# One transposition and four transfers for each unit's maxima, and the last unit's staging two slots later

## The reference, cut to what matters

```python
# x: (2, 512, 128); context: (2, 32, 128); 16 heads of 64
ln = layernorm(layernorm(x));  xn = layernorm(context)
q  = rmsnorm(ln @ Wq) * scale                 # per head
k, v = concat([xn @ Wkv, ln @ Wkv])           # 32 context keys + 512 own keys
attn = softmax(q @ k.T)                       # (2, 16, 512, 544)
x  = x + tanh(g_xattn) * ((attn @ v) @ Wout + bout)
# then 8 experts, top 2 of them, each silu(y @ W_gate) * (y @ W_up) @ W_down
x  = x + tanh(g_ffn) * experts(layernorm(x))
```

## Time and profile before

| | |
|---|---|
| time of three runs, median | 338.35 us (338.27 to 339.49) |
| time of the profiled execution | 338.54 us |
| its span | 336.7 us |
| PE busy | 295.9 us, 88% |
| DVE busy | 276.1 us, 82% |
| POOL busy | 267.5 us, 79% |
| ACT busy | 203.4 us, 60% |
| mean granted clock of PE | 0.976 |

### The profile page before, as it was taken

The page is one execution under the profiler, slowest core; times in us unless marked ns, Lnnn a source line. Parts: engine busy times, 40 slices in busy tenths (PEclk is TensorE's granted clock), DMA queues, the critical chain, the costliest instruction groups (busy, mean ns, idle before and its releaser), DMA issues.

```text
span 336.7 us, 8703 instructions
## 1 busy us (share of the span) xinstructions
PE 295.9 (88%) x3313; PEld 182.0 (54%) x3313; DVE 276.1 (82%) x524; ACT 203.4 (60%) x353; POOL 267.5 (79%) x202
## 2 busy tenths in 40 slices
PE   0466578899999999999999999899988899999993
PEld 0243243455556555565555656677865675655552
DVE  3898888899899898998998986964727976898995
ACT  2463756768756765766766656466673557665551
POOL 8699897897998999999989987545973449677662
PEclk9996969999999999999999999999999999999998
DMA  6405326343514516306308159360100000001001
GB/s 169 136 22 132 67 39 128 43 115 86 122 34 88 126 30 138 84 18 154 75 15 188 51 146 189 102 182 2 45 6 3 0 3 0 2 3 32 2 0 33
DMA packets 33865, 23.63 MB, mean 70 GB/s; under 512 B 10976, under 2 KB 33312, under 8 KB 33824
## 3 DMA queue, kind: packets, MB, share of 16 engines
q1 hardware_dynamic: 32880, 23.03, 29.3%
q10 hardware_dynamic: 944, 0.04, 0.2%
HBM read 5.88 MB, written 0.52 MB: 19 GB/s over the span
## 4 chain that ended last, share of the span: by engine, by line
POOL 34%; PE 24%; issue 20%; DVE 16%; ACT 4%; DMA 1%; POOLq 1%; DVEq 0%; ACTq 0%
POOL p_lo L602 14%; POOL rms_r L501 7%; POOL p_lo L637 7%; PE pj L1348 4%; DVE nm_main L1000 3%; PE big L1537 3%; PE big L1538 2%; PE o_ps L1377 2%; PE tv L1331 2%; PE o_ps L1371 1%; POOL x_sb L647 1%; PE o_ps L1372 1%; DVE wqkv_hl L1238 1%; POOL ln_r L490 1%; DVE qk L981 1%
## 5 line engine op out<-in xcount | busy, mean ns | idle before, releaser
L602 POOL TENSOR_TENSOR p_lo<-p 128x1024 f16<-128x1024 f32 x64 | 121.8, 1915 | 12.8 <-ACT p L798 12.8
L798 ACT ACTIVATE p<-big 128x1024 f32<-128x1024 f32 x64 | 65.6, 1025 | 42.6 <-PE big L1538 42.5
L1000 DVE TENSOR_REDUCE nm_main<-big 128x2 f32<-128x1024 f32 x64 | 78.1, 1220 | 14.1 <-PE big L1396 13.8
L501 POOL TENSOR_TENSOR rms_r<-meansq,power 128x8 f32<-128x8 f32 x32 | 52.3, 1638 | 11.4 <-DVE meansq L974 11.3
L637 POOL TENSOR_TENSOR p_lo<-p,p_lo 128x512 f16<-128x512 f32 x32 | 37.1, 1159 | 30.1 <-ACT p_lo L879 29.2
L1537 PE MATMUL big<-w 128*128 128x512 f16 x128 | 48.8, 381 | 1.9 <-ACT p L798 1.6
L1538 PE MATMUL big<-w 68*128 68x512 f16 x128 | 48.7, 380 | 0.0
L1371 PE MATMUL o_ps<-v,p 128*128 128x65 f16 x512 | 40.3, 193 | 0.0
L1372 PE MATMUL o_ps<-v,p 128*128 128x64 f16 x512 | 40.2, 194 | 0.0
L1371 PEld LDWEIGHTS o_ps<-v,p 128*128 128x128 bf16 x512 | 35.6, 99 | 6.7 <-issue 3.4
L1372 PEld LDWEIGHTS o_ps<-v,p 128*128 128x128 bf16 x512 | 34.1, 97 | 3.1
(11 more groups left out here) (226 smaller groups left out, 713.3 us busy)
## 6 DMA issues: line engine op xcount, KB each, us to landing
w<-hl SPq DMA_DIRECT2D x32, 256.0 KB, 4.1
w<-hl SPq DMA_DIRECT2D x32, 128.0 KB, 3.7
pc_st<-pc_hi SPq DMA_DIRECT2D x64, 32.0 KB, 1.9
pc_st<-pc_lo SPq DMA_DIRECT2D x32, 32.0 KB, 1.8
hl<-n_kernel_gating_EDF_dram SPq DMA_DIRECT2D x1, 1024.0 KB, 6.4
hl<-L_ffn_kernel_up_EDF_dram SPq DMA_DIRECT2D x1, 1024.0 KB, 5.7
o_sb<-in_L_xattn_Wkv_dram SPq DMA_DIRECT2D x2, 384.0 KB, 7.2
x_sb<-in_x_dram SPq DMA_DIRECT2D x2, 256.0 KB, 4.1
```

The lines of the kernel that those rows point to most:

```text
L501: nc.gpsimd.tensor_tensor(rms_r[:, tau % QT, :], meansq[:, tau % QT, :], power[:, 0:8], ALU.pow).then_inc(rr_ok, 1)
L602: nc.gpsimd.tensor_tensor(p_lo[m % NP][:, :], p[m % NP][:, :], p_hi[m % NP], ALU.subtract).then_inc(plo_ok, 1)
L798: nc.scalar.activation(p[n % NP][:, :], st_ps, ACT.Exp).then_inc(exp_ok, 1)
L1000: nc.vector.tensor_reduce(nm_main[:, u % 2, 2 * c:2 * c + 2, q], s2_ps.rearrange("p (k n) -> p k n", k=2), AX_X, ALU.max, negate=True).the ...
```

## The change

`nm16` is turned by one transposition of 128 x 16 in place of four of 128 x 4. The result has 16 rows (4 blocks x 4 heads) of 128, and `nmT` is a tensor of 16 rows; ACT copies 16 x 128 in place of 4 x 512. As the four blocks now lie on different partitions, SP spreads them with four transfers in place of one, and all waits on `sh_ok` count four times as much. Besides, the staging of unit 7 moves from slot 48 to slot 50. In SP's list it comes then behind the stack of unit 6 (slot 49) and still ahead of the transfer of `wd` (slot 51).

```diff
-        nmT = sb("nmT", [HG, QT, P], F16)
+        nmT = sb("nmT", [QT * HG, P], F16)
-        W_AT = {(FIRST, -1)[u] if u < 2 else 8 * u - 8: u for u in range(UNITS)}
+        W_AT = {(FIRST, -1)[u] if u < 2 else 8 * u - (8 if u < UNITS - 1 else 6): u for u in range(UNITS)}
...
-                    sp.dma_start(W2[u % 2][DH:M_ROWS, 2:4, :, :].rearrange("p a e n -> p (a e) n"),
-                                 nmT[:, :, :].rearrange("p q c -> p (q c)").unsqueeze(1).broadcast_to([HG, HG, N])
-                                 ).then_inc(sh_ok[u % 2], 16)
+                    for q in range(QT):
+                        sp.dma_start(W2[u % 2][DH:M_ROWS, 2:4, :, q * P:(q + 1) * P].rearrange("p a e n -> p (a e) n"),
+                                     nmT[q * HG:(q + 1) * HG, :].unsqueeze(1).broadcast_to([HG, HG, P])
+                                     ).then_inc(sh_ok[u % 2], 16)
...
-                    act.wait_ge(sh_ok[(u - 1) % 2], 16 * ((u - 1) // 2 + 1))
-                nc.scalar.copy(nmT[:, :, :], o_ps[0][0:HG, 0:256].bitcast(F16).rearrange("p (q c) -> p q c", c=P)
-                               ).then_inc(nmc_ok, 1)
+                    act.wait_ge(sh_ok[(u - 1) % 2], 16 * QT * ((u - 1) // 2 + 1))
+                nc.scalar.copy(nmT[:, :], o_ps[0][0:QT * HG, 0:P // 2].bitcast(F16)).then_inc(nmc_ok, 1)
...
-                for q in range(QT):
-                    last = nc.tensor.transpose(o_ps[0][0:HG, 64 * q:64 * (q + 1)].bitcast(F16), nm16[:, q, :],
-                                               ident_h[:, :])
-                last.then_inc(nmT_ok, 1)
+                nc.tensor.transpose(o_ps[0][0:QT * HG, 0:P // 2].bitcast(F16), nm16[:, :, :].rearrange("p q h -> p (q h)"),
+                                    ident_h[:, :]).then_inc(nmT_ok, 1)
...
-                    pe.wait_ge(sh_ok[u % 2], 16 * (u // 2 + 1))
+                    pe.wait_ge(sh_ok[u % 2], 16 * QT * (u // 2 + 1))
```

## The result

| | kernel before | kernel after |
|---|---|---|
| time, median (lowest to highest) | 338.44 us (338.27 to 339.49) | 347.52 us (346.66 to 349.6) |
| profiled execution, its own time | 338.54 us | 349.6 us |
| its span | 336.7 us | 347.7 us |
| granted TensorE clock, mean of the span | 0.976 | 0.952 |

The changed kernel is slower: the ratio of the times is 1.0278, with a 95% interval of 1.024 to 1.0315, so about 9.1 us. 345.7 us was predicted, with 342.5 to 348.8 as the range.

What follows compares the result with a forecast made beforehand. PE bounds the stage from 220 to 244, and `wd` lands just as ACT wants it. 338.54 - 0.3 (maxima) + 5.8 (pause) + 1.9 (clock) = 345.9 us, 0.2 above the median, so 345.7 us; range 342.5 to 348.8.

Steps and rivals of the forecast that it cites:

- The mechanism: `wd` is issued behind the staging, 5.75 us later; ACT's split in slot 53 waits, and PE stands ahead of slot 55.
- The stack's wait: PE's 1.05 us wait for unit 6's stack in slot 51 goes, but what is won before slot 53 counts for nothing.
- The term of the pause: PE stands from 224.8 to 230.6 ahead of slot 55, waiting for ACT's exponential: 5.8 us (4.5 to 8).
- The prediction's 0.6 us: Added to the 7.5 us landing of `wd`, as the last staging transfers are still under way; bounds 0 to 1.6 us.
- upper end of 1.6 us: Landing delay of `wd` if it moves nothing before the last staging transfers are done.
- the rule on ring order: Each DMA engine takes one queue's descriptors in ring order; by it `wd` stands fully behind the staging, the 1.6 us end.
- The term of the clock: After PE's pause, some 4 us at the lower clock with half the work done: +1.9 us (0 to 2.5).
- "The clock holds": Rival: PE is fully busy up to the pause, so its clock doesn't fall; 343.8 us, chance 0.22.
- The gain of 0.3 us for the maxima: One transposition for four on PE saves 0.15 us per unit, counted for the last two units only: 2 x 0.15.
- that `wg` is pushed by the four transfers for nothing: In unit 6 `wg` is pushed some 1.7 us; ACT first reads it 8 us after its new issue, so no cost.
- The rival of late transfers in every unit: Slot 8u waits for the four maxima transfers, 0.8 us in five middle units, besides the stall; 349.7 us, chance 0.06.
- 0.90 for slower: Chance that the whole kernel gets slower by more than about 0.5% (1.7 us).

Runs made afterwards that it cites:

- `wd_late`: Kernel before with only the issue of `wd` moved from slot 51 to slot 54, behind unit 7's maxima; 346.26 us, ratio 1.023.
- `stage_only`: Kernel before with only the staging of unit 7 moved from slot 48 to slot 50, maxima as before; 347.92 us, ratio 1.0278.
- `four_others`: Kernel before, four transpositions kept, with four maxima transfers in every unit but unit 6; 338.92 us, ratio 1.0009.
- `maxima_only`: Kernel after with the staging back in slot 48, so one transposition and four transfers in every unit; 342.57 us, ratio 1.0114.
- `four_unit6`: Kernel before, four transpositions kept, with four maxima transfers in unit 6 only; 341.89 us, ratio 1.0107.
- `wd_ahead`: Kernel after with `wd` issued in slot 50 ahead of unit 7's staging, no longer in slot 51; 341.38 us, ratio 1.0074.
- `wd_ahead_stage`: `stage_only`, with the old maxima, and `wd` issued in slot 50 ahead of unit 7's staging; 340.89 us, ratio 1.0057.
- `warm`: Kernel after with 30 matmuls, whose results nobody reads, issued by PE ahead of slot 55; 345.26 us, ratio 1.0199.
- `split_later`: Kernel after, SP's order untouched, with ACT's and DVE's splits of `wd` and `wu` four slots later; 343.71 us, ratio 1.0135.
- `wd_between`: Kernel after with `wd` issued in the midst of unit 7's staging, after its first four transfers; 342.19 us, ratio 1.0084 without the longest execution.

## Why the prediction was right, and where not

**The mechanism held, step by step.** L444 is issued four times in each unit, ahead of the staging; the staging follows the stack; `wd` goes out at 222.5 (the trace is 0.9 us late there, so 221.5 against 220.9 predicted, inside 220.3 to 222.2); the gap on ACT in slot 53 ends with its landing; PE stands ahead of slot 55; the clock is at 0.50 after it. `wd_late` shows that the lateness of `wd` is enough, `stage_only` that the other part of the change has no share in it that the times show.

**The stack's wait went, and was worth nothing.** L1377 of slot 51 has no wait left (before: 1.05 us; with the same order of staging and stack it was 0.6 us in `four_others` and `wd_late` lists none, so it varies from trace to trace):

```profile
211.85 0.28 PE L1377 MATMUL o_ps<-vst,pc_st 96*128 96x65 f16 x4
```

Less the 0.9 us that the trace is late, PE came to the last piece of slot 54 (L1331, 224.04 against 224.39 before) 1.2 us earlier than before, and waited 1.2 us longer for a landing that its own pace doesn't move.

**The term of the pause was sized too small by 1.3 us** (7.1 against 5.8). Half of it, 0.6, is the issue: the stack did not begin 0.3 us earlier, and with 8.6 us (207.09 to 215.65) it took as long as the disturbed one of before (8.5), not the 7.7 taken; the staging gave 0.65 of that back (6.25 us, 215.77 to 222.02, and not 6.9). The other half, 0.65, is the landing: 8.75 us where 8.1 was taken, inside the ends of 7.5 and 9.1. Why it took so long is less plain than my step had it. Landings of `wd` over all the traces, by what was issued around it:

| issued ahead of `wd` | issued directly behind it | us to landing |
|---|---|---|
| the stack | nothing for 5 us | 7.5 (before), 7.0, 6.4, 6.0 (`four_others`, `maxima_only`, `four_unit6`) |
| one maxima transfer | `wu` | 6.4 (`wd_late`) |
| the stack | the staging | 6.8, 7.4 (`wd_ahead`, `wd_ahead_stage`) |
| the staging | one maxima transfer | 7.2 (`stage_only`) |
| the staging | four maxima transfers | 8.75, 8.4, 8.1 (after, `warm`, `split_later`) |
| half the staging | the other half | 8.8 (`wd_between`) |

Behind the staging alone it took 7.2 us, no more than in the quiet case, whose spread is 1.5 us. The prediction's 0.6 us and its upper end of 1.6 us for standing behind the staging were worked out from no row, and this row shows neither. I had read the upper end out of the rule on ring order of the Trainium skill ("DMA: Bandwidth & Descriptors", Queues, rings and completion order). Added to the quiet rows it would give 7.6 to 9.1 us, against the 7.2 of the one trace that has this order; the rule says in what order an engine takes the descriptors of a queue, and no time. The rows of 8 us and more have either the four maxima transfers right behind `wd` or staging on both sides of it. `stage_only` and after differ by the maxima alone, so the table suggests the four transfers as the cause; with one trace against three, and a spread of 1.5 us in the quiet case, that is not shown.

**The term of the clock was sized a little too small,** 2.3 to 2.7 us by the medians and 1.4 to 3.0 in single traces, against 1.9 (2.5 at most). I had taken some 4 us at the lower level from the one fall in the trace of before; from PE's restart it was 3.2 us in `stage_only` and 6.4 us in after. "The clock holds" fell: it went even though PE was fully busy right up to the pause.

**The gain of 0.3 us for the maxima is there, though not where it was expected.** PE's four transpositions shrank from 0.32 to 0.16 us ahead of the next matmul (219.87 to 220.03 in after), and ACT's copy from 572 to 254 ns. Two exponentials of ACT around unit 6's maxima, in before and then in after, stand 2.77 and 2.60 us apart:

```profile
193.47 1.02 ACT L798 ACTIVATE p<-big 128x1024 f32<-128x1024 f32 x1 [1.11 <-PE big L1538]
196.24 1.02 ACT L798 ACTIVATE p<-big 128x1024 f32<-128x1024 f32 x1 [0.41 <-PE big L1538]
```

```profile
194.55 1.02 ACT L798 ACTIVATE p<-big 128x1024 f32<-128x1024 f32 x1 [1.10 <-PE big L1536]
197.15 1.02 ACT L798 ACTIVATE p<-big 128x1024 f32<-128x1024 f32 x1 [0.72 <-PE big L1536]
```

A like step stands at unit 1: the exponentials of after are 1.22 us late at 73.62 (72.40 before) and 1.07 us late at 77.37 (76.30 before). At the units between, 0.15 us is won and lost again in the next slot. All six traces with one transposition show both steps, and none of the six with four does. So 2 x 0.15 was right in size, but the units are 1 and 6 and not the last two, which is luck. The medians can't show 0.3 us: after and `stage_only` have the same ratio, 1.0278, with intervals of 0.3% to each side, and in the traces `wd` takes 1.5 us longer to land in after. The two misses, +1.3 for the pause (read in the longest of the runs) and +0.4 to +0.8 for the clock, are 1.7 to 2.1 us together, against a miss of 1.8.

**A step that failed, though the sum doesn't show it:** that `wg` is pushed by the four transfers for nothing. I asked who waits for `wg`, and in fact nobody did; but I did not ask what is queued behind it. In the old order that is the staging and then the stack, whose wait already stood open, and there the four transfers cost 3.4 to 3.7 us (`four_unit6`, `maxima_only`). In the new order the same push falls into time in which SP is idle and waits for ACT's context exponentials (199.8 to 207.1 in after), as the staging is no longer there, and costs nothing. So the two parts of the change are not independent: the later staging does pay for the four transfers, but it costs 9 us to do so. The rival of late transfers in every unit is refuted by `four_others`; unit 6's own slot 48 starts at 201.05, no later than the 0.9 us that the trace is late anyway.

**Chances.** 0.90 for slower was well placed. The range held the time with 1.3 us to spare above and 5 below. The sizes missed on the same side. For the stack and the landing I had taken values near the undisturbed rows, for a moment that is a disturbed one.

## What to carry to other kernels

An in-order queue of transfers is a resource like an engine: for each issue that is added or moved, list all that is queued behind it, to the end of the stage, and check each one's reader, not only the reader of the one that was moved. A transfer whose landing falls at the very moment of its reader's start is the signature to look for, in two timelines laid side by side; and where the reader is one small instruction on an in-order engine, whatever stands behind it inherits the wait. When the pause hits the matmul engine, add the clock's fall as a term of its own, and measure it with unread matmuls in the gap.

## What was not expected of the hardware

- **Issues get longer when a large transfer is under way.** Four maxima transfers take 2.83 us in unit 6, and directly behind `wd` 4.28 us in after, 3.91 in `warm` and 4.59 in `split_later`; the longest single issue of after is 2.2 us against a median of 0.65. This is L445 of after, ns min/median/max of one:

```profile
L445 SPq DMA_DIRECT2D w<-nmT x32: 637/654/2207, 49.9 to 226.9; - x32
```

- **The landing of a transfer depends on what is under way around it, by amounts that decide here.** `wd` took 6.0 to 8.8 us (the table above); a large staging transfer 4.1 us in the median of before, but 5.1 and 6.1 for the last two of unit 7, and 5.78 for the last of `wd_ahead`; the small lo part of the stack 1.8 us, and 5.28 behind the staging in `four_unit6`.
- **The clock fell after pauses of 1.8 to 2.8 us** in `wd_ahead_stage`, `maxima_only`, `split_later`, `four_unit6` and `wd_ahead` (the stretch 214 to 216 of `maxima_only` is at 0.50), while pauses of 1.05 us in before and 1.6 us in `warm` passed without a fall. Whether anything but the pause had a part in these falls wasn't tried. A small wait can thus cost more than its length: with 1.4 us more of waiting in its trace `maxima_only` is 3.7 us slower.
- **One kernel's executions differ by a fall of the clock near the start,** which is there or not (in two traces of twelve); in the trace of after that was 1.0 us, of the order of the effects that one would like to read. Before unit 1 the twelve traces differ by 3.0 us in all. Late parts of two traces should be compared after the shift that their starts already have.
